# Attention row maxima: from 128-row products one head after the other to 64-row products of two heads side by side

## What is computed

```
xn = layernorm(x)
q, k, v = (xn @ Wq), (xn @ Wk), (xn @ Wv)        # each as 16 heads of 64
scores  = einsum('bqhd,bkhd->bhqk', q, k) * 64 ** -0.5
attn    = softmax(scores, axis=-1)
out     = einsum('bhqk,bkhd->bqhd', attn, v) @ Wo + bo
```

## Time and profile before

| what | value |
|---|---|
| median of 3 runs | 1500.65 us (1494.28 to 1501.56) |
| profiled execution, first to last instruction (span) | 1494.8 us |
| PE busy | 1450.1 us (97%), 6444 instructions |
| DVE busy | 1259.4 us (84%), 1252 instructions |
| POOL busy | 794.5 us (53%) |
| ACT busy | 680.9 us (46%) |
| granted TensorE clock, mean over the span | 0.989 of 2.4 GHz |

### The profile page before, as it was taken

How to read it: one execution, slowest core, us unless ns; L and a number is a source line. 1 busy time by engine, 2 the same in 40 slices (tenths; PEclk the granted TensorE clock), 3 DMA queues, 4 the chain that set the end, 5 groups by cost and what they waited for, 6 DMA issues and landing times.

```text
span 1494.8 us, 23270 instructions
## 1 busy us (share of the span) xinstructions
PE 1450.1 (97%) x6444; PEld 844.8 (57%) x6444; DVE 1259.4 (84%) x1252; ACT 680.9 (46%) x1286; POOL 794.5 (53%) x607
## 2 busy tenths in 40 slices
PE   5889999999999999999999999999999999999998
PEld 3545655556655566555565556656556555555543
DVE  7788888888898888888889888898888888889965
ACT  4244444444444444444444444444444444444443
POOL 8285554555544555554555554555544554467555
PEclk9799999999999999999999999999999999999999
DMA  2333110331121311213112131122201220001000
GB/s 78 85 89 92 38 40 27 79 84 23 38 61 48 83 38 26 59 45 84 40 31 71 39 73 40 39 67 70 57 18 40 66 66 22 22 14 37 1 15 15
DMA packets 66100, 73.25 MB, mean 49 GB/s; under 512 B 8992, under 2 KB 39072, under 8 KB 65952
## 3 DMA queue, kind: packets, MB, share of 16 engines
q1 hardware_dynamic: 64928, 69.44, 18.9%
q0 software_dynamic: 1024, 2.10, 0.5%
HBM read 18.42 MB, written 5.24 MB: 16 GB/s over the span
## 4 chain that ended last, share of the span: by engine, by line
PE 86%; DVE 10%; issue 3%; POOL 1%; DMA 0%; ACT 0%; SPq 0%; POOLq 0%; DVEq 0%; ACTq 0%
PE OB L947 29%; PE SB L918 17%; PE SB L922 14%; PE MB L935 14%; DVE acc L655 3%; DVE mx L639 3%; DVE rd L760 2%; PE XB L993 2%; PE XB L975 2%; PE XB L984 1%; PE XB L902 1%; PE XB L909 1%; PE XB L954 1%; PE XB L956 1%; PE XB L955 1%
## 5 line engine op out<-in xcount | busy, mean ns | idle before, releaser
L400 POOL TENSOR_TENSOR acc<-acc,ex 128x512 f32<-128x512 f32 x448 | 600.3, 1340 | 549.5 <-ACT ex L497 548.5
L497 ACT ACTIVATE ex<-SB 128x512 f32<-128x512 f32 x1024 | 556.3, 595 | 651.1 <-PE SB L922 644.1
L639 DVE TENSOR_REDUCE mx<-MB 128x1 f32<-128x1024 f32 x512 | 618.5, 1214 | 197.5 <-PE MB L935 194.8
L947 PE MATMUL OB<-ex,V 128*64 128x512 f32 x2048 | 497.6, 605 | 0.0
L655 DVE TENSOR_TENSOR acc<-acc,ex 128x512 f32<-128x512 f32 x448 | 469.6, 1048 | 12.3 <-ACT ex L497 11.7
L918 PE MATMUL SB<-Q,K 128*128 128x512 f32 x1024 | 440.6, 430 | 4.3 <-issue 3.9
L922 PE MATMUL SB<-Q,K 128*128 128x512 f32 x1024 | 403.8, 394 | 0.0
L918 PEld LDWEIGHTS SB<-Q,K 128*128 128x128 f32 x1024 | 192.6, 188 | 254.4 <-issue 208.4
L935 PE MATMUL MB<-K,Q 128*128 128x512 f32 x1024 | 285.2, 399 | 7.3 <-DVE mx L639 5.7
L947 PEld LDWEIGHTS OB<-ex,V 128*64 128x64 f32 x2048 | 126.8, 136 | 230.2 <-issue 199.3
L935 PEld LDWEIGHTS MB<-K,Q 128*128 128x128 f32 x1024 | 192.6, 190 | 57.7 <-DVE mx L639 12.0
(11 more groups left out here) (121 smaller groups left out, 585.8 us busy)
## 6 DMA issues: line engine op xcount, KB each, us to landing
Q<-qhi SPq DMA_DIRECT2D x124, 128.0 KB, 2.3
K<-khi SPq DMA_DIRECT2D x112, 128.0 KB, 2.3
Q<-qlo SPq DMA_DIRECT2D x64, 128.0 KB, 2.3
K<-klo SPq DMA_DIRECT2D x56, 128.0 KB, 2.4
w<-fc SPq DMA_DIRECT2D x24, 256.0 KB, 2.7
w<-projT SPq DMA_DIRECT2D x24, 256.0 KB, 3.1
sorted_x<-res SPq DMA_DIRECT2D x1, 1536.0 KB, 7.2
tok<-sorted_x SPq DMA_DIRECT2D x24, 64.0 KB, 1.7
```

The costliest lines, as they stand in the source:

```text
L400: pool.tensor_tensor(a[:, :], src[:, :], EX[1][kt % RING][:, :], ALU.add).then_inc(g_a, 1)
L497: act.activation(EX[h][kt % RING][:, :], SB[h][:, :], ACT.Exp).then_inc(a_e, 1)
L639: dve.tensor_reduce(mx[:, m % 2, u:u + 1], MB[i % 2][:, :], AX.X, ALU.max).then_inc(v_m, 1)
L947: mm = pe.matmul(OB[own[h], :], V[(n // JB) % 2][:, k, own[h]], EX[h][k % RING][:, :], start=(k == 0), stop=(k == NT - 1))
```

## The change

The products for the row maxima use only the head's own 64 partitions: high q times high k, without the rest of q. `max_unit` becomes `max_pair`: it issues two units at a time, one of each head, for the same queries and the same half of the keys. Head 0 reads partitions 0 to 63 (the upper half of the array's rows) and writes `MB[0]`, head 1 reads partitions 64 to 127 and writes `MB[1]`; the four matmuls go head 0, head 1, head 0, head 1. A pair waits for both banks at once, that is until DVE has reduced all units before it. `column` maps the new order of units to the same columns of `mx`. At the start, the first pair no longer waits for the DMAs into the other halves but for ACT's copies alone, and the wait for these DMAs (`k_ready`) moves to the first scores.

```diff
--- before.py
+++ after.py
@@ -235,7 +235,18 @@
         START = [SB[0], SB[1], OB, XB]
         TX = [MB[j % 2][:, j // 2 * QB:(j // 2 + 1) * QB] for j in range(JB)]
-        ORDER = list(range(0, UNITS, 2)) + list(range(1, UNITS, 2))
+        def at_start(g):
+            return g % TB, g // TB
+        def later(g):
+            return g // 2, g % 2
+        def column(i, order):
+            q, half = order(i // 2)
+            return (i % 2) * (UNITS // 2) + 2 * q + half
         LAST = [SB[0], SB[1], MB[0][:, 0:QB], MB[1][:, 0:QB]]
@@ -632,9 +643,9 @@
             @block.vector
             def _(dve):
-                def maxima(m, i, u=None):
-                    u = i if u is None else u
+                def maxima(m, i, order=later):
+                    u = column(i, order)
                     wait(dve, t_m, m.times(UNITS, i + 1))
                     dve.tensor_reduce(mx[:, m % 2, u:u + 1], MB[i % 2][:, :], AX.X, ALU.max).then_inc(v_m, 1)
@@ -783,7 +794,7 @@
                         if s_ == 3:
                             low_q0()
                     for u in range(UNITS):
-                        maxima(Lin(0), u, ORDER[u])
+                        maxima(Lin(0), u, at_start)
                         if u in BETWEEN:
                             kind, c = BETWEEN[u]
                             if kind == "q":
@@ -915,26 +926,29 @@
                         wait(pe, a_e, n.times(2 * NT, 2 * kt + h - 1))
                         if kt == 0:
                             q_ready(pe, n)
+                            if n.i is None and n.off == 0:
+                                k_ready(pe, n)
                         pe.matmul(SB[h][:, :], K1[par][h][:, keys], Q1[k][h][:, :], start=True, stop=False)
                         if kt == 0 and h == 0:
                             wait(pe, d_nm[k], (n // JB).times(32, 32))
                             wait(pe, g_c, 1)
                         pe.matmul(SB[h][:, :], K2[par][h][:, keys], Q2[k][h][:, :], start=False, stop=True).then_inc(t_s, 1)
-                def max_unit(m, i, u=None):
-                    u = i if u is None else u
-                    h, q, half = u // 8, u % 8 // 2, u % 2
-                    par, k = (m // JB) % 2, m % JB
-                    wait(pe, v_m, m.times(UNITS, i - 1))
-                    if i == 0 and (m.i is not None or m.off):
+                def max_pair(m, g, order=later):
+                    q, half = order(g)
+                    par, k, rows = (m // JB) % 2, m % JB, slice(q * P, (q + 1) * P)
+                    wait(pe, v_m, m.times(UNITS, 2 * g))
+                    if g == 0 and (m.i is not None or m.off):
                         q_ready(pe, m)
                         k_ready(pe, m // JB)
                     for c in range(2):
                         keys = slice((2 * half + c) * QB, (2 * half + c + 1) * QB)
-                        mm = pe.matmul(MB[i % 2][:, c * QB:(c + 1) * QB], Q1[k][h][:, q * P:(q + 1) * P],
-                                       K1[par][h][:, keys], start=True, stop=True)
-                    mm.then_inc(t_m, 1)
+                        for h in range(2):
+                            mm = pe.matmul(MB[h][:, c * QB:(c + 1) * QB], Q1[k][h][own[h], rows],
+                                           K1[par][h][own[h], keys], start=True, stop=True)
+                            if c == 1:
+                                mm.then_inc(t_m, 1)
                 def times_v(n, kt, tiles):
@@ -1011,23 +1025,23 @@
                             pe.wait_ge(g_lo, j)
                             make_kv("k", Lin(0), j - 1, START[j - 1])
                     pe.wait_ge(a_x, JB)
-                    pe.wait_ge(d_q0, 32)
-                    for u in range(UNITS):
-                        if u in (0, UNITS // 2):
-                            for c in (0, 1) if u == 0 else (2, 3):
-                                pe.wait_ge(d_k0[c], 32)
-                        max_unit(Lin(0), u, ORDER[u])
-                        if u in BETWEEN:
-                            kind, c = BETWEEN[u]
-                            if kind == "v":
-                                make_kv("v", Lin(0), c)
-                            elif kind == "q":
-                                make_q(Lin(c))
-                            else:
-                                logits(c)
+                    pe.wait_ge(a_q, 1)
+                    for g in range(UNITS // 2):
+                        if g % TB == 0:
+                            pe.wait_ge(a_k, 2 + g // 2)
+                        max_pair(Lin(0), g, at_start)
+                        for u in (2 * g, 2 * g + 1):
+                            if u in BETWEEN:
+                                kind, c = BETWEEN[u]
+                                if kind == "v":
+                                    make_kv("v", Lin(0), c)
+                                elif kind == "q":
+                                    make_q(Lin(c))
+                                else:
+                                    logits(c)
                     turn_max(Lin(0))
-                    for u in range(LEAD):
-                        max_unit(Lin(1), u)
+                    for g in range(LEAD // 2):
+                        max_pair(Lin(1), g)
                 def one(n):
                     start = n.i is None and n.off == 0
@@ -1037,9 +1051,10 @@
                         scores(n, kt)
-                        for m, u in (unit(n, kt - 1), unit(n, kt)) if kt % 2 else ():
+                        if kt % 2:
+                            m, u = unit(n, kt - 1)
                             if before(m, NB):
-                                max_unit(m, u)
+                                max_pair(m, u // 2)
                         if kt == AT_DEN and not start:
                             denominators(n - 1)
                         if start and kt == AT_RANK:
```

## The result

The changed kernel takes 1505.7 us (median, 1505.1 to 1507.2) where the kernel before takes 1500.1: ratio 1.0043, 95% interval 1.0027 to 1.0060. Run once more beside later experiments it gave 1505.6, ratio 1.0043 (1.0028 to 1.0057). So it is 6 us slower, not 12 us faster. The profiled execution of the changed kernel has a span of 1504.2 us, that of before 1494.8.

The account below looks back on a forecast made before the run. PE was taken as the bound nearly everywhere; 16.2 gained in pairs, less 1.3 near the end and 3 at the start, gives 12 us: 1500.65 - 12 = 1488.6, so 1488.5 us, range 1405 to 1522.

Parts of the forecast that it names:

- PE is the bound: Whole kernel: PE sets the pace nearly everywhere, DVE has about 7 us of room per block; the change works on 236 us.
- (1): Max matmuls: four 128-row matmuls become four 64-row ones running side by side in row halves, 0.46 instead of 0.92 us.
- (2): Entry and exit of each pair: two more changes of the array's shape, emptying plus uncovered weight loads, 0.39 us together.
- (3): Sum of a pair on PE: 0.46 + 0.39 = 0.85 against 0.92 us, a gain of 0.07 us.
- (4): Pairs that count: 231 of 256 gain 0.07 each, 16.2 us; seven others lose 0.19 each, 1.3 us.
- (5): Wait for both banks in the steady part: costs nothing; DVE gets a pair's first unit about 0.2 us later.
- (6): Start, where DVE is the bound: needing both banks at once leaves DVE gaps, net +3 us, between +1 and +5.
- Rival D: Lower granted clock in the longer waits of the start: some 2 us more, within the start's bounds; no chance of its own.
- The end: Seven pairs between 1340 and 1422 us already wait for DVE: no gain, 1.3 us lost to the exit's switch.
- The distance of 5.85 us between span and median: Run median lies 5.85 us above the profiled span; kept unchanged to turn the forecast span into a time.
- rival C: Max matmul pairs: halves overlap but not fully, a pair costs 0.96 us or more; 1514 to 1522 us, chance 0.17.
- within: Outcome for the whole kernel: time within 0.5% (7.5 us) of no change, chance 0.14.

Follow-up runs that it names:

- e9: e7 with the four products of every pair (from block 1's fifth unit on) issued twice into the same banks: 1581.5 us, 102.8 more than e7.
- e7: Changed kernel with the wait of e1 and the start of the kernel before (128 rows, unit by unit, its DMA waits): 1478.7 us, ratio 0.9875.
- e6: Kernel before with POOL's first addition of each block waiting for VectorE's first: 1491.6 us, ratio 0.9957.
- e1: Changed kernel with POOL's first addition of each block waiting for VectorE's first: 1481.6 us, ratio 0.9892 to the kernel before.
- e8: e1 with products of 128 rows in place of the 64-row ones, and the DMA waits of the kernel before at the start: 1495.8 us, ratio 0.9994.
- e4: Kernel before with the wait for both banks: the first unit of each two waits for all reductions before it: 1505.3 us, ratio 1.0041.
- e10: Changed kernel with the start of the kernel before (128 rows, unit by unit, its DMA waits), nothing else: 1500.5 us, ratio 1.0009.
- e2: Kernel before with VectorE's first addition of each block waiting for POOL's first: 1499.3 us, ratio 0.9999.
- e12: The changed kernel run and profiled once more, nothing altered: 1505.6 us, ratio 1.0043 to the kernel before.
- e3: Changed kernel with its 64-row products at the start issued unit by unit, each waiting for its own bank alone: 1505.9 us, ratio 1.0048.

## Why the prediction was wrong

- *PE is the bound, the pair's matmuls are 236 us of it*: right; chain and e9 agree.
- *(1) Row halves run side by side*: right, 0.23 us a round for both heads (e9: 0.46 for two rounds).
- *(2) Four pieces of switch, 0.39 us*: right. The pair and the score product behind it went from 1.15 to 1.09 us. The rule of the Trainium skill that a change of tiling mode empties the array ("TensorEngine Tiling (Array Packing)", Key Properties) holds here for row halves too: 0.36 us of idle loads on either side.
- *(3), (4) 0.07 per pair, 231 pairs, 15 us net*: right as the worth of the products, 0.062 (e7 against e6) and 0.068 per pair (e1 against e8), 12.9 and 14 to 15 us in all, wherever nothing else gave way.
- *(5) "DVE gets the first unit of a pair about 0.2 us later than now, ... inside the same room"*: this is the step that failed. The delay was sized right (0.26 us at the place above), and the room of 7 us per block was there. But I measured the room only between the last reduction and the next pair. I had not asked what else is queued on VectorE behind the reductions in step 2: an addition that went 0.05 us ahead of POOL's, and then the reciprocal, for which PE waits with the bank XB. Losing that order cost 0.93 us on VectorE and, with the delay itself, the whole gain. The forecast wanted 45.01 - 0.56 = 44.45 us per block and got 45.07, which is 13 us over the 21 steady blocks; with the order held (e1) they take 44.27, since that also mends the blocks in which the kernel before had lost it (e6). The rows that would have warned are the two additions of the timeline of before (927.84 and 927.89, 0.68 and 1.75 us) and every fourth block, in which POOL is first and PE already waits.
- *(6) The start, +3, between +1 and +5*: the mechanism was right (both banks at once, VectorE is the bound there, and the DMA wait removed brings nothing: the first reduction is at 25.50 instead of 25.62). The size was off: 6.5 us. The gap at full clock was right (0.82 in e4), and with the gap at that size e4 is still 5.4 us late. What failed is "in about half of them": I took half of the seven gaps as hidden behind VectorE's other work, but its waits between the reductions of block 0 add up to 9.4 us in the changed kernel and to 2.8 in the kernel before. Rival D, the lower clock, makes gaps of 1.31 us and is about 1 us of the total, within the 2 that I had put on it.
- *The end*: small, as forecast.
- *The distance of 5.85 us between span and median*: it was 1.5 in the changed kernel.
- The range held the time, but that is luck: the forecast's own range ended at 1497, and it was rival C, which didn't happen, that stretched the whole to 1522. (Its upper end is also added up wrong: 1514 + 0.05 x 231 is 1526.) Of the chances, "within" 7.5 us of no change, put at 0.14, came out, by a flipped order on VectorE and POOL that none of the rivals named.

**Open.** Blocks 10 and 18, where PE's loop of eight blocks turns, took 93.6 us before and 96.8 after, and between 93.5 and 98.5 in the others with single pairs, and the granted clock goes with it: a stretch of 3.4 us at the lower level stands in the longer of a kernel's two (in the changed kernel block 10 with 49.0 us; block 18, without it, has 47.8), in both for e1 and e10, and in neither for the kernel before, e2 and e6. It isn't fixed by the program: the changed kernel profiled again (e12) has it in block 18 (49.5) and not in block 10 (47.4). In the kernels before and changed PE stands idle for 1.85 to 2.65 us at each turn, with nothing in the profile that it waits for. I haven't tested what decides it. Nor have I tested why e3's start stayed slow.

## What to carry to other kernels

A change that makes one engine's work ready 0.2 us later can be far inside that engine's room and still cost more than it brings, if a queue behind it holds something that races another engine for the same resource: look for pairs of instructions that start within a tenth of a microsecond of each other and have uneven lengths. Such an order should be fixed by a semaphore rather than left to the last 50 ns; here one wait was worth 24 us in one kernel and 6 in the other. And when a total agrees with a theory (e4 did, to 0.4 us), compare it stretch by stretch before believing it.

## What was not expected of the hardware

- Additions of 128 x 512 in fp32 on VectorE and POOL don't run side by side: with VectorE first by 0.05 us they take 0.68 and 1.75 us, with POOL first by 0.21 us 1.61 and 1.27. The second one loses more time on VectorE (0.93 us) than on POOL (0.48). With POOL first, VectorE's ends at a fixed time whenever it started: behind by 0.18, 0.21, 0.44, 0.69 and 0.75 us it took 1.63, 1.61, 1.38, 1.13 and 1.07, each time 1.81 to 1.82 us from POOL's start, 0.55 behind POOL's end (kernels before and changed). The Trainium skill, "SBUF — State Buffer", section SBUF: two separate sides, says that a VectorE instruction with two inputs in SBUF and a GpSimd instruction that reads SBUF share a port pair as an exclusive lock, which whichever starts first holds for the whole instruction; by that rule both timelines agree, but for the second one's record ending 0.13 to 0.15 us sooner than its length alone would put it.
- Changing from whole-array products to row halves and back costs 0.09 to 0.10 us of emptying and 0.10 of uncovered weight load each way, much as for column halves (there the load of 64 columns on the way in is about 0.05), and it eats five sixths of the halved matmul time at 512 columns and two rounds per visit.
- Weight loads of 128 columns into two row halves don't queue behind each other: four of 0.19 us in 0.30 us, the two of a round starting 3 to 4 ns apart.
